# Gated window attention on one Trainium2 core: values projected in front of the row products, and eight-row turns of the maxima

## The chip, the cores and the metric

The kernel runs on 1 core of one Trainium2 (trn2) chip. The metric is the device time in microseconds (us) of one execution. Before the change the median of 3 runs is 1691.44 us (1687.55 to 1694.93).

## What is computed

Eight batches of 512 positions with 256 channels. Each is normalised, projected to 32 query heads and 8 key and value heads of 64, turned by a rotary embedding, and goes through attention in a window of 128 positions to either side with a sink logit for each head. The result is projected back, multiplied by a gate from a small layer with an 8-bit float input, and added to x.

```
xn = layernorm(x)
q, k, v = xn@Wq + bq, xn@Wk + bk, xn@Wv + bv            # q: 32 heads, k and v: 8 heads
q, k = rope(q)*SCALE, rope(k)*SCALE
scores = where(|i - j| <= 128, q.k, -1e9)
probs = softmax(concat(scores, sink))[..., :-1]
s = (probs @ v) @ Wo + bo
scale = max(max(|xn|) / 448, 1e-7)                      # over all eight batches
g = silu(float8((xn / scale)) @ weight.T + bias)
out = x + s * g
```

## The kernel before, in words

The program is written out by hand for each engine; the order of each engine's work is that of its own `step` function, and semaphores order the engines among each other. There are 64 steps, one for each batch n and key head k (step `it` is 8n + k), each with its 4 query heads. A step has 4 slots (q = 0 to 3), one for each tile of 128 query positions. Three stages overlap: in slot q of step `it` TensorE

- projects the queries of step it+2 (`queries`, slot 0 only, two times six matmuls, L1171),
- computes the scores of step `it`, tile q, transposed, in blocks of 128 keys (`scores`, L1253 and L1255; ScalarE takes the exponential of each block, L676, and GpSimd cuts the window's edge, L580),
- computes row products of step it+1 (`score_rows`, L1229, called `row(h)` for the 4 heads), of which VectorE takes the largest value of each row (`maximum`, L988),
- multiplies the exponentials of the tile before with the values (`weighed(h)`, L1269: two blocks of keys make 4 records, three make 6), and VectorE divides by the sums (`normalised`, L997 to L1003),
- turns the heads of the tile before that (`heads_turn`, L1279, two transposes into bank ring[2]), ScalarE and VectorE split the result into a high and a low part (`o_high` L734, `o_low` L1009), and the tile before that one is projected back (`out_project`, L1294).

The softmax needs the maxima as rows that a matmul can add. So two tiles' maxima (4 heads each) are negated (L729), turned by a matmul each into ring[2] (`turn_max`, L1203, in slots 1 and 3), and ScalarE writes 4 rows of 256 columns for each head into `qT_high` (`max_rows`, L711), each with the column of the identity that keeps one head's row and zeroes the others. The second half of `scores` then has 64 + 4 rows. Ring[2] serves both turns: `heads_turn` waits in slots 1 and 3 until `max_rows` has read it, and ScalarE runs `max_rows` in order behind two exponentials.

Once in a while a slot has other work (`chunk_at`): keys of a coming group of four heads, the values of the coming batch (`project_values`, L1180, slots 1 to 3 of step 7, and slot 1 of step 0 for the last tile), transposes of x. In those slots the heads go in the order 0, 2, 1, 3. The values' bank is ring[1], which `row(1)` and `row(3)` also use. `row(0)` of tile 0 waits for the q and k of the step it belongs to, which arrive by DMA.

The opening (step -1) prepares the first batch, surveys all the other batches for the largest |x| (`survey`, `widest`, VectorE and GpSimd), and computes the scale from it. Here the values of tiles 0 to 2 are projected in slots 1 to 3, each ahead of its slot's row products, and VectorE adds their bias ahead of its maxima.

```
                    if it == -1:
                        extra()
                    row(0)
```

## Time and profile before

| | |
|---|---|
| median of 3 runs | 1691.44 us |
| profiled execution, own time | 1689.69 us |
| its span, first to last instruction | 1687.8 us |
| TensorE busy | 1623.2 us, 96% of the span |
| VectorE, ScalarE, GpSimd busy | 68%, 59%, 62% |
| mean granted TensorE clock | 0.979 of full speed |
| one batch (eight steps), from 501 to 702 us | 201 us |

The span is that of the profiled execution; 1.9 us of its time lie around it. PE is TensorE, PEld its weight loads, DVE VectorE, ACT ScalarE, POOL GpSimd. A PE record's own duration includes its way through the array; how much of PE's time it takes is read from the start of one to the start of the next. From about 105 us on the profile repeats with every batch, and ahead of that lies the opening.

### The profile page before, as it was taken

The page shows a single profiled execution, that of the slowest core. Times are in us where ns is not written, and L with a number is a line of the kernel's source. Part 1 is how long each engine was busy: PE and PEld are TensorE (multiplying, and loading weights), DVE is VectorE, ACT ScalarE, POOL GpSimd, SP SyncE. Part 2 cuts the span into 40 slices and gives each one's busy share as a digit, 9 for nine tenths or more (in the row PEclk, how much of TensorE's full clock was granted, in tenths as well). Part 3 has the DMA queues.
Part 4 walks back from the last instruction along what each step waited for, and adds up shares of the span by engine and source line. Part 5 has one row for each costly group of instructions (what it writes and reads, how often), then busy time and mean ns, then how long its engine had stood idle before and what let it go on. Part 6 is the DMA issues. An engine that isn't in the chain of part 4 may idle for free.

```text
span 1687.8 us, 34027 instructions
## 1 busy us (share of the span) xinstructions
PE 1623.2 (96%) x11139; PEld 1459.4 (86%) x11139; DVE 1140.4 (68%) x3619; ACT 991.3 (59%) x2407; POOL 1039.2 (62%) x1016
## 2 busy tenths in 40 slices
PE   3699999999999999999999999999999999999998
PEld 2498988999898998988989898898988899898987
DVE  8656776766766766666676667676676667666664
ACT  2346665566565665566655666556655566555663
POOL 5647675675666666575576666566665666656651
PEclk8679999999999999999999999999999999999999
DMA  6535535435444453534545443643544544443550
GB/s 205 129 73 102 93 69 104 86 78 98 76 88 97 83 98 71 107 70 85 97 77 100 82 88 72 113 82 74 107 72 83 102 77 98 79 79 76 94 97 13
DMA packets 77277, 150.87 MB, mean 89 GB/s; under 512 B 12720, under 2 KB 25264, under 8 KB 73008
## 3 DMA queue, kind: packets, MB, share of 16 engines
q1 hardware_dynamic: 77104, 148.71, 45.6%
q8 instruction: 91, 1.49, 0.4%
q14 instruction: 82, 0.67, 0.2%
HBM read 18.64 MB, written 4.19 MB: 14 GB/s over the span
## 4 chain that ended last, share of the span: by engine, by line
PE 90%; issue 3%; ACT 3%; DVE 2%; POOL 1%; DMA 1%; SPq 0%; POOLq 0%; DVEq 0%; ACTq 0%
PE pv_bank L1269 30%; PE ring L1171 13%; PE ring L1229 11%; PE acc L1294 10%; PE score L1253 9%; PE score L1255 8%; PE ring L1279 4%; PE ring L1180 3%; PE ring L1161 1%; PE ring L1203 1%; ACT qT_high L711 1%; ACT prob_all L676 1%; DMA gate<-in_w_all 1%; PE ring L1141 0%; DVE k_first_hi L966 0%
## 5 line engine op out<-in xcount | busy, mean ns | idle before, releaser
L988 DVE CUSTOM_DVE_ANT_0 junk<-ring,mask,sink 128x384 bf16<-128x384 f32 (+1 forms) x1024 | 558.7, 549 | 306.8 <-PE ring L1229 288.4
L1269 PEld LDWEIGHTS pv_bank<-v,prob_all 128*128 128x128 f32 x5120 | 689.2, 193 | 31.2 <-ACT prob_all L676 11.6
L1269 PE MATMUL pv_bank<-v,prob_all 128*128 128x65 f32 x5120 | 690.9, 266 | 3.6 <-DVE o_norm L1003 1.4
L580 POOL TENSOR_SCALAR_AFFINE_SELECT prob_all<-prob_all 128x512 f32<-128x512 f32 x384 | 255.6, 680 | 456.9 <-ACT prob_all L676 456.9
L676 ACT ACTIVATE prob_all<-score 128x512 f32<-128x512 f32 x640 | 371.5, 596 | 183.1 <-PE score L1255 172.3
L1229 PE MATMUL ring<-kT_high,qT_full 128*128 128x384 f32 (+1 forms) x1024 | 373.3, 365 | 22.6 <-issue 12.0
L1253 PE MATMUL score<-qT_full,kT_high 128*128 128x512 f32 x640 | 265.0, 414 | 0.7
L1255 PE MATMUL score<-qT_high,kT_low 68*128 68x512 f32 x640 | 255.5, 399 | 0.0
L1229 PEld LDWEIGHTS ring<-kT_high,qT_full 128*128 128x128 f32 x1024 | 197.5, 193 | 56.4 <-issue 15.6
L734 ACT ACTIVATE oT_hi<-ring 128x256 fp32r<-128x256 f32 x256 | 96.7, 378 | 179.6 <-PE ring L1279 178.6
L1009 DVE TENSOR_TENSOR oT_lo<-ring,oT_hi 128x256 fp32r<-128x256 f32 x256 | 107.9, 422 | 137.1 <-ACT oT_hi L734 135.4
L711 ACT ACTIVATE qT_high<-ring,ident 4x256 fp32r<-4x256 f32 x512 | 196.4, 452 | 5.9 <-PE ring L1203 2.6
L1294 PE MATMUL acc<-wo_hi,oT_hi 128*128 128x256 f32 x512 | 155.4, 304 | 0.2 <-DVE oT_lo L1009 0.2
L540 POOL TENSOR_TENSOR q_first<-q_first,q_first_hi 128x512 f32<-128x512 f32 x64 | 83.8, 1309 | 115.6 <-ACT q_first_hi L693 115.6
L1294 PE MATMUL acc<-wo_hi,oT_lo 128*128 128x256 f32 x512 | 143.4, 280 | 0.0
L1294 PE MATMUL acc<-wo_lo,oT_hi 128*128 128x256 f32 x512 | 143.3, 280 | 0.0
L1171 PE MATMUL ring<-xT_hi,w_hi 128*128 128x512 f32 x320 | 129.5, 405 | 12.3 <-ACT q_even L682 8.3
L1253 PEld LDWEIGHTS score<-qT_full,kT_high 128*128 128x128 f32 x640 | 122.3, 191 | 15.3 <-ACT prob_all L676 1.8
L1171 PE MATMUL ring<-xT_hi,w_lo 128*128 128x512 f32 x320 | 127.5, 398 | 0.0
L1171 PE MATMUL ring<-xT_lo,w_hi 128*128 128x512 f32 x320 | 127.3, 398 | 0.0
L1255 PEld LDWEIGHTS score<-qT_high,kT_low 68*128 68x128 f32 x640 | 121.9, 191 | 2.7
L682 ACT ACTIVATE q_even<-ring,q_bias 128x512 f32<-128x512 f32 x64 | 44.1, 689 | 129.9 <-PE ring L1171 129.9
(127 smaller groups left out, 2570.2 us busy)
## 6 DMA issues: line engine op xcount, KB each, us to landing
qT_high<-qT_full SPq DMA_DIRECT2D x64, 512.0 KB, 4.5
qT_full<-q_first SPq DMA_DIRECT2D x64, 256.0 KB, 4.2
qT_full<-q_first_hi SPq DMA_DIRECT2D x64, 256.0 KB, 5.5
qT_full<-q_second SPq DMA_DIRECT2D x64, 256.0 KB, 4.2
qT_full<-q_second_hi SPq DMA_DIRECT2D x64, 256.0 KB, 5.4
kT_high<-k_first_hi SPq DMA_DIRECT2D x128, 64.0 KB, 2.5
kT_high<-k_second_hi SPq DMA_DIRECT2D x128, 64.0 KB, 2.7
x_res<-in_x SPq DMA_DIRECT2D x10, 512.0 KB, 6.2
```

Source lines behind the costliest of these rows:

```text
L580: nc.gpsimd.affine_select(out=pr, in_=pr, compare_op=ALU.is_ge, fill=0.0, base=0, pattern=[[0, GROUP], [sign, P]], channel_multiplier=-sign) \
L676: nc.scalar.activation(prob[:, q % 2 * 3 + n, :], score[(FIRST[q] + n) % 2][:, :], ACT.Exp) \
L711: last = nc.scalar.activation(qT_high[D:D + NR, s % 2, h, pair * 2 * P:(pair + 1) * 2 * P], ring[2][0:NR, 0:2 * P], ACT.Copy, scale=ident[ ...
L734: nc.scalar.activation(oT_hi[:, q % 2, :], ring[2][:, 0:KT * P], ACT.Copy).then_inc(s_oT_hi_done, 1)
L988: nc.vector.tensor_tensor_reduce(junk[:, h % 2, 0:cols], ring[h % 2][:, 0:cols], mask[:, m0:m0 + cols], 1.0, sink[:, col:col + 1], ALU.add ...
L1009: nc.vector.tensor_tensor(oT_lo[:, q % 2, :], ring[2][:, 0:KT * P], oT_hi[:, q % 2, :].bitcast(F32), ALU.subtract).then_inc(s_oT_lo_done, 1)
L1171: last = nc.tensor.matmul(bank[:, :], w[:, k, col:col + P], xs[:, k, :], start=(n == 0), stop=(n == len(products) - 1))
L1229: nc.tensor.matmul(ring[h % 2][:, 0:cols], qT_full[:, b % 2, h, q * P:(q + 1) * P], kT_high[:, b % 3, k0 * P:k0 * P + cols], start=True, s ...
L1253: nc.tensor.matmul(score[blk % 2][:, :], kT_high[:, c % 3, k * P:(k + 1) * P], qT_full[:, c % 2, :, q * P:(q + 1) * P], start=True, stop=F ...
L1255: nc.tensor.matmul(score[blk % 2][:, :], kT_low[0:D + NR, c % 3, k * P:(k + 1) * P], qT_high[0:D + NR, c % 2, :, q * P:(q + 1) * P], start ...
L1269: last = nc.tensor.matmul(pv[:, h, :], prob[:, q % 2 * 3 + n, h * P:(h + 1) * P], v[:, slot, k, :], start=(n == 0), stop=(n == len(BLOCKS[ ...
L1294: last = nc.tensor.matmul(acc[q // 2][:, (q % 2) * M:(q % 2 + 1) * M], left[:, q % 2, k * P:(k + 1) * P], right[:, col:col + M], start=fre ...
```

## The change

Four things change.

1. The maxima of two tiles are turned by one matmul into eight rows (`NR` is 8). `max_rows` then issues eight ACTIVATEs of 8 rows by 128 columns where it issued four of 4 by 256. `scores` has 72 rows in its second half.
2. In slots 1 and 3 `heads_turn` follows `weighed(3)`; VectorE's `normalised` goes ahead of `o_low` there, and in slot 1 ahead of `maximum` 3.
3. In slot 1 of step 7 TensorE projects the values ahead of `row(0)`, and VectorE adds their bias ahead of that row's maximum.
4. In the opening the values of tiles 0 to 2 are projected at once into ring[1], score[0] and score[1], ahead of all row products, and their bias is added ahead of all maxima. 32 matmuls whose result nobody reads (`turn_over`) stand ahead of step -1, and 12 behind the values.

```diff
-NR = GROUP
+NR = 2 * GROUP
@@ max_rows (ACT)
-                for h in range(GROUP):
-                    last = nc.scalar.activation(qT_high[D:D + NR, s % 2, h, pair * 2 * P:(pair + 1) * 2 * P],
-                                                ring[2][0:NR, 0:2 * P], ACT.Copy, scale=ident[0:NR, h:h + 1])
+                for t in range(2):
+                    for h in range(GROUP):
+                        i, q = t * GROUP + h, 2 * pair + t
+                        last = nc.scalar.activation(qT_high[D:D + NR, s % 2, h, q * P:(q + 1) * P],
+                                                    ring[2][0:NR, 2 * P:3 * P], ACT.Copy, scale=ident[0:NR, i:i + 1])
@@ step (DVE)
-                    if it < 0 and other is not None:
-                        values(other[1], other[2])
+                    if (it, q) == (-1, 0):
+                        for t in range(TILES - 1):
+                            values(0, t)
+                    first = (k, q) == (KV - 1, 1) and it >= 0 and other is not None
+                    if first:
+                        values(other[1], other[2])
...
-                    if real(back(it, q, 2)[0]):
+                    if q % 2 == 0 and real(back(it, q, 2)[0]):
                         o_low(*back(it, q, 2))
+                    if q == 1 and real(back(it, q, 1)[0]):
+                        normalised(*back(it, q, 1))
                     if real(r) and order[1] == 2 and q < 3:
                         maximum(r, tile, 3, order)
-                    if real(back(it, q, 1)[0]):
+                    if q != 1 and real(back(it, q, 1)[0]):
                         normalised(*back(it, q, 1))
+                    if q % 2 and real(back(it, q, 2)[0]):
+                        o_low(*back(it, q, 2))
@@ turn_max (PE)
-                for t in range(2):
-                    last = nc.tensor.matmul(ring[2][0:NR, t * P:(t + 1) * P], neg_parts[:, pair, t, :], ident_r[:, :],
-                                            start=True, stop=True)
-                last.then_inc(s_max_turned_pe, 1)
+                nc.tensor.matmul(ring[2][0:NR, 2 * P:3 * P], neg_parts[:, pair, :], ident_r[:, :],
+                                 start=True, stop=True).then_inc(s_max_turned_pe, 1)
@@ step (PE)
-                    if it == -1:
-                        extra()
-                    row(0)
+                    first = (k, q) == (KV - 1, 1) and it >= 0 and other is not None
+                    if not first:
+                        row(0)
...
+                    if it == -1 and q == 0:
+                        pe.wait_ge(s_odd_done, 2)
+                        project_values(0, ring[1])
+                        project_values(1, score[0])
+                        project_values(2, score[1])
+                        turn_over(12)
                     maxima_turn()
                     if heads_at(it, q)[1] == 2:
                         if it >= 0:
                             extra()
+                        if first:
+                            row(0)
                         weighed(0)
                         third()
                         row(2)
                         weighed(1)
                         row(1)
                         weighed(2)
-                        heads_turn()
                         if q == 3:
                             row(3)
                             weighed(3)
+                            heads_turn()
+                        elif q == 1:
+                            weighed(3)
+                            heads_turn()
+                            row(3)
                         else:
+                            heads_turn()
                             weighed(3)
                             row(3)
...
+            def turn_over(count):
+
+                for _ in range(count):
+                    nc.tensor.matmul(acc[1][:, :], ident_r[:, :], xT_hi[:, 0, :], start=True, stop=True)
```

TensorE, slot 1 of a step without other work (step 3 of the first batch). Names are tiles: `ring<-kT_high,qT_full` is a row product, `ring<-ident,o_norm` the turn of the heads, `pv_bank` the product with the values. Before:

```order
L1229 MATMUL ring<-kT_high,qT_full 128x256 [waits max_done]
L1269 MATMUL pv_bank<-v,prob_all 128x65 x2
L1229 MATMUL ring<-kT_high,qT_full 128x256 [waits max_done]
L1269 MATMUL pv_bank<-v,prob_all 128x65 x2
L1279 MATMUL ring<-ident,o_norm 128x128 [waits oT_lo_done,norm_done,max_rows_done]
L1279 MATMUL ring<-ident,o_norm 128x128
L1269 MATMUL pv_bank<-v,prob_all 128x65 x2
L1294 MATMUL acc<-wo_hi,oT_hi 128x256 [waits oT_lo_done]
```

and of the change, at the same place:

```order
L1246 MATMUL ring<-kT_high,qT_full 128x256 [waits max_done]
L1288 MATMUL pv_bank<-v,prob_all 128x65 x2
L1246 MATMUL ring<-kT_high,qT_full 128x256 [waits max_done]
L1288 MATMUL pv_bank<-v,prob_all 128x65 x4
L1298 MATMUL ring<-ident,o_norm 128x128 [waits oT_lo_done,norm_done,max_rows_done]
L1298 MATMUL ring<-ident,o_norm 128x128
L1313 MATMUL acc<-wo_hi,oT_hi 128x256 [waits oT_lo_done]
```

The turn of the maxima, some rows above, was two matmuls (L1203, 4x128 each) and is one (L1219, 8x128). The last head's product with the values stands ahead of the heads' turn instead of behind it.

TensorE, slot 1 of step 7 in the first batch, before:

```order
L1255 MATMUL score<-qT_high,kT_low 128x512
L1229 MATMUL ring<-kT_high,qT_full 128x256 [waits kT_high_in,max_done,qT_second_in,qT_first_in]
L1253 MATMUL score<-qT_full,kT_high 128x512 [waits exp_done]
L1255 MATMUL score<-qT_high,kT_low 128x512
L1203 MATMUL ring<-ident_r,neg_parts 4x128 [waits max_rows_done,neg_done,oT_lo_done]
L1203 MATMUL ring<-ident_r,neg_parts 4x128
L1180 MATMUL ring<-w_hi,xT_hi 128x512 [waits max_done]
```

and of the change:

```order
L1274 MATMUL score<-qT_high,kT_low 128x512
L1219 MATMUL ring<-ident_r,neg_parts 8x128 [waits max_rows_done,neg_done,oT_lo_done]
L1192 MATMUL ring<-w_hi,xT_hi 128x512 [waits max_done]
L1192 MATMUL ring<-w_lo,xT_hi 128x512
L1192 MATMUL ring<-w_hi,xT_lo 128x512
L1192 MATMUL ring<-w_hi,xT_hi 128x512
L1192 MATMUL ring<-w_lo,xT_hi 128x512
L1192 MATMUL ring<-w_hi,xT_lo 128x512
L1246 MATMUL ring<-kT_high,qT_full 128x256 [waits kT_high_in,max_done,qT_second_in,qT_first_in]
L1288 MATMUL pv_bank<-v,prob_all 128x65 [waits norm_done,cut_done,exp_done]
```

The row product that waits for the DMAs of q and k stands behind both scores, the turn of the maxima and the six matmuls of the values.

VectorE in the opening, of the change, behind the sixth survey (`L977` and `L980` are the values' bias, `L992` the maxima, `L845` the seventh survey):

```order
L852 BN_AGGR x_moments<-stats 128x2 [waits row_bn] x4
L977 TENSOR_TENSOR v<-ring,v_bias 128x7x64 [waits v_pe]
L980 TENSOR_TENSOR v<-ring,v_bias 128x64
L977 TENSOR_TENSOR v<-score,v_bias 128x7x64 [waits v_pe]
L980 TENSOR_TENSOR v<-score,v_bias 128x64
L977 TENSOR_TENSOR v<-score,v_bias 128x7x64 [waits v_pe]
L980 TENSOR_TENSOR v<-score,v_bias 128x64
L992 ISA junk,row_max<-ring,mask,sink 128x256 [waits max_pe]
L992 ISA row_max 128x1
```

The three values stand in a row ahead of the first maximum; before, each stood ahead of the four maxima of its slot.

## Rows read from the trace of the kernel before

**Rows 1.** The page, part 1: each engine's busy time

```profile
PE 1623.2 (96%) x11139; PEld 1459.4 (86%) x11139; DVE 1140.4 (68%) x3619; ACT 991.3 (59%) x2407; POOL 1039.2 (62%) x1016
```

**Rows 2.** Busy time by stretch: opening, cold stretch, one batch (PE, PEld, DVE, ACT, POOL, PEclk)

```profile
44.75:62.53 17.78, 12.09 (x25) 7.14 (x25) 12.32 (x43) 7.62 (x16) 17.26 (x12) 0.50 0.96 203
82.00:100.00 18.00, 18.00 (x76) 16.50 (x77) 7.18 (x27) 7.64 (x19) 10.59 (x11) 0.50 0.13 22
501.00:702.00 201.00, 199.14 (x1393) 180.06 (x1393) 138.04 (x443) 122.17 (x300) 127.04 (x124) 1.00 0.46 87
```

**Rows 3.** Waits of TensorE from 110 to 1680 us: total us, times, longest

```profile
PE ring L1229 <- issue: 8.4, 7, 2.1
```

**Rows 4.** Timeline, PE, slot 1 of a plain step: start us, duration us

```profile
517.85 0.55 PE L1269 MATMUL pv_bank<-v,prob_all 128*128 128x65 f32 x4
518.37 0.44 PE L1279 MATMUL ring<-ident,o_norm 128*128 128x128 f32 x2
518.64 0.56 PE L1269 MATMUL pv_bank<-v,prob_all 128*128 128x65 f32 x4
519.01 0.37 PE L1294 MATMUL acc<-wo_hi,oT_hi 128*128 128x256 f32 x1
```

**Rows 5.** Timeline, ACT, the same slot

```profile
516.78 1.53 ACT L711 ACTIVATE qT_high<-ring,ident 4x256 fp32r<-4x256 f32 x4
```

**Rows 6.** Timeline, ACT, the two smallest copies of 128 columns

```profile
4.51 0.31 ACT L647 ACTIVATE ident_b<-ident 128x128 bf16<-128x128 f32 x1 [2.44 <-POOL mask L491]
4.73 0.29 ACT L648 ACTIVATE ident_r<-ident 128x128 fp32r<-128x128 f32 x1
```

**Rows 7.** Groups of ACT by shape: busy us, mean ns of one

```profile
L676 ACT ACTIVATE prob_all<-score 128x512 f32<-128x512 f32 x640 | 371.5, 596 | 183.1 <-PE score L1255 172.3
L711 ACT ACTIVATE qT_high<-ring,ident 4x256 fp32r<-4x256 f32 x512 | 196.4, 452 | 5.9 <-PE ring L1203 2.6
L720 ACT ACTIVATE sink_exp<-neg_parts,sink 128x2 f32<-128x2 f32 x512 | 108.2, 285 | 0.1
...
L682 ACT ACTIVATE q_even<-ring,q_bias 128x512 f32<-128x512 f32 x64 | 44.1, 689 | 129.9 <-PE ring L1171 129.9
```

**Rows 8.** Timeline, ACT, slot 3 of a plain step

```profile
503.67 1.53 ACT L711 ACTIVATE qT_high<-ring,ident 4x256 fp32r<-4x256 f32 x4
```

**Rows 9.** Timeline, PE, the same slot 3

```profile
505.50 0.39 PE L1279 MATMUL ring<-ident,o_norm 128*128 128x128 f32 x2
```

**Rows 10.** Timeline, PE, slot 1 of a step 7

```profile
461.32 0.40 PE L1255 MATMUL score<-qT_high,kT_low 68*128 68x512 f32 x1
462.77 0.36 PE L1229 MATMUL ring<-kT_high,qT_full 128*128 128x256 f32 x1 [1.05 <-issue]
...
463.43 0.28 PE L1203 MATMUL ring<-ident_r,neg_parts 128*4 128x128 f32 x2
463.55 0.44 PE L1180 MATMUL ring<-w_hi,xT_hi 128*128 128x512 f32 x1
...
464.99 0.55 PE L1269 MATMUL pv_bank<-v,prob_all 128*128 128x65 f32 x4
...
465.90 0.28 PE L1229 MATMUL ring<-kT_high,qT_full 128*128 128x256 f32 x1
```

**Rows 11.** Timeline, PE, slot 3 of a step 7

```profile
480.48 0.39 PE L1279 MATMUL ring<-ident,o_norm 128*128 128x128 f32 x2
480.90 0.44 PE L1229 MATMUL ring<-kT_high,qT_full 128*128 128x384 f32 x1
```

**Rows 12.** Timeline, DVE, the opening

```profile
44.75 0.59 DVE L973 TENSOR_TENSOR v<-ring,v_bias 128x448 f32<-128x448 f32 x1
...
45.39 0.47 DVE L988 CUSTOM_DVE_ANT_0 junk<-ring,mask,sink 128x256 bf16<-128x256 f32 x1
...
58.74 0.63 DVE L973 TENSOR_TENSOR v<-ring,v_bias 128x448 f32<-128x448 f32 x1 [3.02 <-PE ring L1180]
```

**Rows 13.** Timeline, POOL, the opening

```profile
55.31 2.28 POOL L507 TENSOR_TENSOR x_rstd<-x_var,minus_half_all 128x12 f32<-128x12 f32 x1
```

More of the change, by code:

```diff
@@ L971, in values @@
                 dve.wait_ge(s_v_pe, TILES * m + t + 1)
+                bank = score[t - 1] if m == 0 and t in (1, 2) else ring[1]
                 last = KV - 1 + m % 2
                 nc.vector.tensor_tensor(v[:, 0:KV - 1, t, 0:D],
-                                        ring[1][:, 0:(KV - 1) * D].rearrange("p (g d) -> p g d", d=D),
+                                        bank[:, 0:(KV - 1) * D].rearrange("p (g d) -> p g d", d=D),
                                         v_bias[:, 0:(KV - 1) * D].rearrange("p (g d) -> p g d", d=D), ALU.add)
-                nc.vector.tensor_tensor(v[:, last, t, 0:D], ring[1][:, (KV - 1) * D:], v_bias[:, (KV - 1) * D:],
+                nc.vector.tensor_tensor(v[:, last, t, 0:D], bank[:, (KV - 1) * D:], v_bias[:, (KV - 1) * D:],
                                         ALU.add).then_inc(s_v_done, 1)
@@ L1091, in step @@
                         beside(it, n, k, q)
-                    if other is not None and it >= 0:
+                    if other is not None and it >= 0 and not first:
                         if other[0] == "k":
@@ L1179, in project_values @@
                 for n, (xs, w, k) in enumerate(products):
-                    last = nc.tensor.matmul(ring[1][:, :], xs[:, k, t * P:(t + 1) * P], w[:, k, W_V:W_V + KV * D],
+                    last = nc.tensor.matmul(bank[:, :], xs[:, k, t * P:(t + 1) * P], w[:, k, W_V:W_V + KV * D],
                                             start=(n == 0), stop=(n == len(products) - 1))
                 last.then_inc(s_v_pe, 1)
+            def turn_over(count):
+                for _ in range(count):
+                    nc.tensor.matmul(acc[1][:, :], ident_r[:, :], xT_hi[:, 0, :], start=True, stop=True)
             def queries(a, odd):
@@ L1214, in score_rows @@
                         pe.wait_ge(s_odd_done, 1)
-                if h == 1:
-                    other = chunk_at(it // KV, it % KV, slot)
+                if h == 1 and b == 0 and q == 0:
+                    pe.wait_ge(s_v_done, 1)
+                elif h == 1:
+                    other = chunk_at(it // KV, it % KV, slot) if it >= 0 else None
                     if slot == 0 and real(it + 2):
@@ L1315, in other_chunk @@
                 elif kind == "v":
-                    if i == 0 and j == 0:
-                        pe.wait_ge(s_odd_done, 2)
-                    if i == 0 and j > 0:
-                        pe.wait_ge(s_v_done, j)
-                    project_values(j)
+                    project_values(j, ring[1])
                 elif kind == "x":
@@ L1446, in _ @@
             queries(0, 1)
+            turn_over(32)
             for it in range(-1, STEPS + 1):
```

16 lines of the change are left out of this document (11 added, 5 removed).

## The prediction

> **What bounds the kernel now.** I read the page first, then the busy time by stretch, then the waits of TensorE, and then the timelines of TensorE, ScalarE and VectorE slot by slot. The page has TensorE busy for 96% of the span, 28 points ahead of VectorE, the next engine [rows 1]. The stretch of one batch says it more sharply: 199.14 of 201 us at the full clock [rows 2]. So from 105 us on every matmul taken away is time gained, as long as no other engine ends the slot, and every wait put into TensorE's stream is lost. The waits have one large entry there: seven times a row product waits for something that is no engine, 8.4 us in all [rows 3]. Those are the DMAs of q at the step between two batches. Small waits hide in the array's tail, so I take them from start to start. In slot 1 of a plain step the third head's product starts at 517.85 and is good for 0.37 us (as the fourth's from 518.64 to 519.01), so the turn of the heads could start at 518.22; it starts at 518.37 [rows 4], just after the last of the four ACTIVATEs that read ring[2] ends (516.78 + 1.53 = 518.31) [rows 5]. So in this slot ScalarE already sets the pace by 0.15 us. The profile shows this in steps 1 to 5 of each batch, 40 slots in all; in slot 1 of steps 0, 6 and 7, with their six extra matmuls, ScalarE is done 0.9 us or more before. Ahead of 105 us VectorE is the bound of the opening: between 44.75 and 62.53 us it is busy 12.32 of 17.78 us, with TensorE at half clock [rows 2].
>
> **One matmul for the turn.** Two matmuls take 0.12 us from 463.43 to 463.55 [rows 10]; one takes 0.06. That saves 0.06 us in 128 turns, but in the 40 slots where ScalarE sets the pace it saves nothing: 88 x 0.062 = **5.5 us less**.
>
> **Eight ACTIVATEs for four.** No row shows an ACTIVATE of 128 columns with a scale read from memory, one after the other. From four of 256 columns (mean 0.452, four in 1.53) their spacing is (1.53 - 0.45) / 3 = 0.36 us; for 2 columns with a pointer it is (4 x 0.211 - 0.285) / 3 = 0.19 [rows 7]. Half-way between lies 0.28. The other route: a plain copy of 128 columns takes 0.29 to 0.31 with a spacing of 0.22 [rows 6], and a pointer operand adds 0.09 (0.689 for q_even against 0.596 for the exponential, both 512 columns) [rows 7]: 0.29 to 0.31. Bounds: 0.22 if the pointer is free, 0.36 if 128 columns cost as much as 256. I take 0.28, as both routes end near it: 7 x 0.28 + 0.38 = 2.34 us for the eight, 0.81 us more than now. In the 40 slots the last head's product now stands ahead of the turn, so TensorE is ready at 518.22 - 0.06 + 0.37 = 518.53; ScalarE ends at 516.78 + 2.34 = 519.12, so the turn starts at 519.17, and the back projection 0.27 us later at 519.44 instead of 519.01: 0.43 us. **40 x 0.43 = 17.2 us more.** The reordering thus pays 0.37 of the 0.81. In slot 3 ScalarE ends at 505.20 and the turn starts at 505.50 [rows 8, 9]; it moves to 505.50 - 0.06 + 0.59 = 506.03 against 506.01 + 0.05. That is even; in step 6, where the margin is 0.17 instead of 0.30, it lacks 0.15. With rounding in the others: **2 us more**.
>
> What waits behind the longer ACTIVATEs on ScalarE: the third exponential, four small ones for the sinks and the high part of the heads. They come 0.8 us later, and TensorE's next score, 0.4 later as well, finds ScalarE just free. VectorE's `o_low` waits for that high part; that `normalised` now stands ahead of it is what keeps the product's bank from being late. I cost these moves at nothing; if the cover fails, the next maximum is late by some tenths in the same 40 slots.
>
> By the Trainium skill ("ScalarE: Activation LUTs", section on what ACT_TABLE_LOAD costs) an ACTIVATE takes 186 ns + 0.833 ns a column, each pointer operand adds 93 ns, and neighbours overlap by 93 ns. That fits the row of 2 columns (279 + 2 = 281 against 285 ns), while for 256 columns it gives 492 ns against the 452 of the trace. As an estimate by that page, eight of 128 columns take 7 x 0.293 + 0.386 = 2.44 us, and the sum below comes out some 8 us higher.
>
> **Values ahead of `row(0)`, seven times.** The row product starts 1.45 us after the score before it, which needs 0.23: 1.22 us of wait, of which the list shows 1.05 [rows 10]. Over seven that makes 8.4 + 7 x 0.17 = 9.6 us. The second score, the turn and the values (463.55 to 464.99, 1.44 us) now stand there, 1.96 us in all; only the longest wait of 2.1 + 0.17 leaves 0.3. The values move the load: VectorE adds the bias first (44.75 to 45.39, 0.64 us) and then takes the maximum (0.47) [rows 12]. With 0.2 us to start, my estimate, the maximum is there 1.35 us after the values' last matmul. `row(2)`, which needs it, would be ready after row(0)'s 0.12 and the 0.91 from 464.99 to 465.90 [rows 10], 1.03 in all. A new wait of 0.32, seven times 2.3. Net **-9.6 + 0.3 + 2.3, about 6.9 us less**. What is late next here is VectorE.
>
> **Slot 3 with other work (steps 1, 5, 7).** Here row(3) waits for a maximum, and the turn of the heads fills part of that wait: 480.48 to 480.90 is 0.42 us, of which the turn takes some 0.24 (0.27 where it follows a wait) [rows 4, 11]. Behind the change row(3) is issued at the same time, since VectorE sets it, and the turn comes afterwards: 0.24 us in each of 23 such slots, **5.5 us more**.
>
> **The opening.** VectorE idles 17.78 - 12.32 = 5.46 us between 44.75 and 62.53 [rows 2]. 3.02 of it is the wait for tile 2's values, which TensorE projects late and at half clock [rows 12]; the rest is the start of pairs of maxima behind the values. With all values first, both row products are ready when VectorE comes to them. I leave 0.3 for the turn of the first maxima in slot 3: **5.2 us less**. Next in line is GpSimd's last 1/sqrt, done at 55.31 + 2.28 = 57.6 [rows 13]; the new end, 57.3 plus the 1.1 us for the reduction of x, lies behind it. The 44 idle matmuls lie ahead of row products that cannot be served before VectorE is free at 44.75, and I cost them at nothing: 32 of them take 7.4 us (0.23 each) in a wait of over 8. If the clock were at half, values and fillers would end near 49 us, and 2.5 of the 5.2 would be gone.
>
> **Sum.** -5.5 + 17.2 + 2 - 6.9 + 5.5 - 5.2 = +7.1 us. The profiled execution took 1689.7 us, so 1696.8; it lies 1.7 us under the median of the runs, so against the median that is 1698.5. I forecast **1697**. About 0.5%, 8.5 us, is what a measurement of this kernel can tell from no change: the forecast is at the upper edge of no change.
>
> **Rivals.**
> 1. *ScalarE's spacing is 0.29 or more.* One mechanism, in slots 1 of steps 1 to 5 and then in slots 3. For it speak the copies plus pointer. At 0.29 the eight take 2.42 us, 0.08 more: 40 x 0.08 + 32 x 0.08 + 8 x 0.08 = 6.4, in all +13.5: **1703**, slower by 0.8%. The sum passes +8.5 with less than 0.003 us more of spacing than I took. Were it 0.36, it would be 0.6 us more in all 80 slots: some 50 us, which nothing but the bound speaks for.
> 2. *The spacing is 0.22, the pointer free when in a row.* The eight take 1.85; ScalarE ends at 518.63, TensorE waits 0.15 as now and saves the rest. 17.2 and 2 vanish and 2 come back: -14: **1676**, faster by 0.8%. Against it: 0.19 for only 2 columns.
> 3. *The clock.* After the opening TensorE runs at half clock from 82 to beyond 100 us though busy all the time [rows 2], behind a wait of 2.5 us. If other timing of the opening avoids that, the 18 us alone give back 9: **1688**, no change; if it comes once more, 1706.
> 4. *The fillers or the banks do not keep the opening short*: half of the 5.2 lost, **1699.5**.
>
> **Chances.** Forecast and what lies around it 0.42; it lies near the edge, so 0.10 of that is slower and 0.32 within 0.5%. Rival 1 0.22, slower. Rival 2 0.16, faster. Rival 3 0.12, a third each: the better clock with cheap ACTIVATEs (faster), with the forecast's (within), and the worse one (slower). Rival 4 0.08, 0.03 of it slower. That makes faster 0.20, within 0.5% 0.41, slower 0.39. The range from 1680 to 1710 leaves out most of rival 2 and the far end of rival 1, at most 0.2 together.
>
> **What would show it.** The ACTIVATEs of 8 x 128: spacing 0.28, eight in 2.3 us. Slot 1 of steps 1 to 5: turn of the heads 0.6 us behind the last product. Slot 1 of step 7: no wait at row(0), a small one at row(2). Slot 3 of steps 1, 5, 7: 0.24 more before row(3). VectorE from the first value to the reduction of x in 12.6 us instead of 17.8. A batch takes 202.5 us instead of 201. If the eight take under 2.1 us, or the batch is at or below 201, my term for ScalarE is wrong; if the opening gains nothing, the one for VectorE.

## The result and the profile after

| | before | after |
|---|---|---|
| median of 10 runs each, on the same chip | 1688.13 us | 1680.52 us |
| lowest and highest | 1683.89, 1694.93 | 1677.29, 1686.64 |
| ratio to before, 95% interval | | 0.9955 [0.9941, 0.9969] |
| profiled execution (span) | 1689.69 us (1687.8) | 1686.64 us (1684.7) |
| a batch, from `q_even` to `q_even` eight steps later | 201.0 us | 200.1 us |

The change takes 7.6 us off, 0.45%. The forecast was 1697, 0.5% up: the sign is wrong. The profiled execution after is the slowest of its ten, so the two profiled spans differ by 3 us where the medians differ by 7.6. Most of this lies in the first batch, which takes 213.4 us before and 217.4 after, and 207.6 to 220.0 in the profiled executions of the experiments. From the second batch on the traces of both kernels repeat within 0.2 us (but for the seventh before, 202.1 us, with the longest wait for q), so I read the change there.

Two things lengthen the first batch after. When step 1 starts, the changed kernel is 6.4 us ahead (first score at 99.96 against 106.35 us). There VectorE stands for x of the coming batch, `gate` is queued behind that, and TensorE's turn of the heads waits for `gate`; the kernel before comes later and has no such wait of TensorE:

```profile
106.91 0.75 DVE L817 BATCH_NORM_STATS2 stats<-x_in 128x6 f32<-128x256 f32 x2 [5.53 <-DMA x_in<-in_x]
107.58 0.67 DVE L912 TENSOR_TENSOR gate<-ring,ffn_bias 128x512 f32<-128x512 f32 x1
```

```profile
108.31 0.69 PE L1298 MATMUL ring<-ident,o_norm 128*128 128x128 f32 x2 [3.27 <-DVE gate L912]
```

Then the granted clock goes to half from 107.8 to 121.4 us, and slot 1 of step 1 takes 8.64 us instead of 4.89. Nine of the fourteen traces of this document have this wait of TensorE, 2.6 to 3.3 us long.

The page after, part 1 (each engine's busy time; answers to [rows 1]), and part 4 (the chain that ended last) by engine:

```profile
PE 1620.2 (96%) x11055; PEld 1463.0 (87%) x11055; DVE 1151.2 (68%) x3619; ACT 1064.5 (63%) x2919; POOL 1036.7 (62%) x1016
...
PE 80%; ACT 9%; DVE 6%; issue 3%; DMA 1%; POOL 1%; SPq 0%; POOLq 0%; DVEq 0%; ACTq 0%
```

The same line of part 4 before:

```profile
PE 90%; issue 3%; ACT 3%; DVE 2%; POOL 1%; DMA 1%; SPq 0%; POOLq 0%; DVEq 0%; ACTq 0%
```

ScalarE is busy 73 us longer than in [rows 1], and has gone from 3% of the chain to 9%. The chain names a new pacemaker, not a loss: the time fell.

Busy time of the engines after, in a stretch of one batch (columns as in [rows 2]):

```profile
501.00:702.00 201.00, 198.52 (x1388) 180.21 (x1386) 139.80 (x445) 131.81 (x365) 126.55 (x124) 1.00 0.47 88
```

TensorE idles 2.5 us in it, where [rows 2] had 1.9. Waits of TensorE, from 110 to 1680 us (in all, times, longest), after:

```profile
PE ring L1246 <- DVE row_max L992: 6.9, 28, 0.3
PE ring L1298 <- ACT qT_high L713: 4.5, 17, 0.4
PE ring L1246 <- issue: 2.0, 1, 2.0
PE pv_bank L1288 <- DVE o_norm L1007: 1.9, 8, 0.2
```

and two lines of the same list before, beside [rows 3]:

```profile
PE ring L1279 <- ACT qT_high L711: 2.2, 9, 0.3
PE pv_bank L1269 <- DVE o_norm L1003: 1.4, 4, 0.4
```

The wait for q [rows 3] fell from 8.4 us to 2.0. Of its seven places before, six are slot 1 of step 7 (7.2 us), and these are gone; the seventh, and the one that is left, is slot 1 of step 6 in the last batch, where it grew from 1.2 to 2.0. Two small waits came up: one for a maximum, 28 times, and the one for the ACTIVATEs, 17 times where it stood 9 times. A matmul's record runs on while it passes through the array, and a start that is late by less than that tail leaves no idle time in this list. So the ledger is better made slot by slot, from the first score of a slot to the first score of the next, medians over batches 3 to 7 (us):

| slots | before | after | change | forecast |
|---|---|---|---|---|
| slot 1 of steps 1, 3, 4, 5 | 4.89 | 5.02 | +0.13 | +0.43 |
| slot 1 of step 2 | 5.46 | 5.59 | +0.13 | +0.43 |
| slot 2 of steps 2, 3, 4 | 5.95 | 5.65 | **-0.30** | 0 |
| slot 1 of step 7 | 7.39 | 6.52 | -0.87 | -1.0 |
| slot 3 of steps 1, 5 | 8.68 | 8.80 | +0.12 | +0.18 |
| slot 3 of step 7 | 8.43 | 8.55 | +0.12 | +0.18 |
| slot 3 of steps 0, 2, 3, 4 | 6.74 | 6.68 | -0.06 | 0 |
| slot 1 of steps 0, 6 | 6.12, 6.40 | 6.05, 6.33 | -0.07 | -0.06 |

Over all 32 slots of a batch the changes add up to -1.0 us (slot 2 of step 1 rose by 0.10); the period of a batch fell by 0.9.

**Slot 1.** Timeline after, TensorE and then ScalarE, in the slot of [rows 4, 5] (start, duration):

```profile
518.79 1.00 PE L1288 MATMUL pv_bank<-v,prob_all 128*128 128x65 f32 x8
519.94 0.44 PE L1298 MATMUL ring<-ident,o_norm 128*128 128x128 f32 x2
520.13 0.37 PE L1313 MATMUL acc<-wo_hi,oT_hi 128*128 128x256 f32 x1
```

```profile
517.78 2.11 ACT L713 ACTIVATE qT_high<-ring,ident 8x128 fp32r<-8x128 f32 x8
519.91 0.60 ACT L676 ACTIVATE prob_all<-score 128x512 f32<-128x512 f32 x1
```

The group of ACT by shape (busy us, mean ns of one):

```profile
L713 ACT ACTIVATE qT_high<-ring,ident 8x128 fp32r<-8x128 f32 x1024 | 269.9, 343 | 3.3
```

Eight take 2.11 us with a mean of 0.343, so they follow one another at (2.11 - 0.343) / 7 = 0.252 us. The turn starts 0.05 us behind the last, as forecast, but it is 0.23 us less late. The back projection starts 0.19 us behind the turn (519.94, 520.13), where the forecast had 0.27; that is the rest of the difference between +0.13 and +0.43.

**Slot 2, where the forecast has nothing.** VectorE before, then after, at the start of slot 2 of step 2 (its first score starts at 547.44 before, at 548.89 after):

```profile
547.63 0.42 DVE L1009 TENSOR_TENSOR oT_lo<-ring,oT_hi 128x256 fp32r<-128x256 f32 x1 [1.56 <-ACT oT_hi L734]
...
548.37 0.43 DVE L1003 TENSOR_TENSOR o_norm<-pv_bank,rden 128x256 f32<-128x256 f32 x1
```

```profile
548.47 0.42 DVE L1007 TENSOR_TENSOR o_norm<-pv_bank,rden 128x256 f32<-128x256 f32 x1 [0.42 <-PE ring L1298]
549.53 0.42 DVE L1013 TENSOR_TENSOR oT_lo<-ring,oT_hi 128x256 fp32r<-128x256 f32 x1 [0.63 <-ACT oT_hi L737]
```

TensorE before, then after: the second row product of the slot and the first product with the values:

```profile
548.54 0.34 PE L1229 MATMUL ring<-kT_high,qT_full 128*128 128x384 f32 x1
548.94 0.63 PE L1269 MATMUL pv_bank<-v,prob_all 128*128 128x65 f32 x4
```

```profile
550.00 0.34 PE L1246 MATMUL ring<-kT_high,qT_full 128*128 128x384 f32 x1
550.17 0.78 PE L1288 MATMUL pv_bank<-v,prob_all 128*128 128x65 f32 x6
```

Before, VectorE stands for 1.56 us in front of `o_low`, which needs ScalarE's high part, and `o_norm`, which empties the products' bank, is queued behind it. It ends at 548.80, and the first product follows at 548.94, 0.40 us behind the row product, which is good for 0.17. After, `o_norm` is done at the slot's start, and the product follows at 0.17 us. That wait of 0.23 us or more was there in the trace before, and I had not laid VectorE's rows of this slot beside TensorE's. The list of waits has no entry for this slot, but it had a hint: the line on `pv_bank` above names the same pair of VectorE and TensorE, in slot 3 of step 6 of the first batch and at three places of the last.

### The profile page after: what moved, and what is told of

Read it like the earlier page. It is cut to its first block, busy times and chain, and to the rows that moved or that the text cites. A ratio compares the mean times of both kernels' runs of the same rounds, so it can differ in the third digit from the quotient of the medians.

```text
span 1684.7 us, 34367 instructions
## 1 busy us (share of the span) xinstructions
PE 1620.2 (96%) x11055; PEld 1463.0 (87%) x11055; DVE 1151.2 (68%) x3619; ACT 1064.5 (63%) x2919; POOL 1036.7 (62%) x1016
## 4 chain that ended last, share of the span: by engine, by line
PE 80%; ACT 9%; DVE 6%; issue 3%; DMA 1%; POOL 1%; SPq 0%; POOLq 0%; DVEq 0%; ACTq 0%
PE pv_bank L1288 24%; PE ring L1183 13%; PE acc L1313 10%; PE ring L1246 9%; PE score L1272 8%; PE score L1274 7%; ACT qT_high L713 5%; PE ring L1298 4%; ACT prob_all L676 3%; PE ring L1192 2%; DVE junk L992 2%; PE ring L1173 1%; DVE k_first_hi L969 1%; DMA gate<-in_w_all 1%; PE ring L1153 0%
## 5 line engine op out<-in xcount | busy, mean ns | idle before, releaser
L992 DVE CUSTOM_DVE_ANT_0 junk<-ring,mask,sink 128x384 bf16<-128x384 f32 (+1 forms) x1024 | 561.1, 550 | 318.7 <-PE ring L1246 300.2
L1288 PE MATMUL pv_bank<-v,prob_all 128*128 128x65 f32 x5120 | 677.8, 267 | 1.9 <-DVE o_norm L1007 1.9
L713 ACT ACTIVATE qT_high<-ring,ident 8x128 fp32r<-8x128 f32 x1024 | 269.9, 343 | 3.3
L1274 PE MATMUL score<-qT_high,kT_low 72*128 72x512 f32 x640 | 256.6, 401 | 0.0
L1274 PEld LDWEIGHTS score<-qT_high,kT_low 72*128 72x128 f32 x640 | 123.0, 192 | 2.9
L1007 DVE TENSOR_TENSOR o_norm<-pv_bank,rden 128x256 f32<-128x256 f32 x256 | 108.7, 425 | 16.9 <-PE ring L1298 9.2
```

Of the source, the lines that this page charges most:

```text
L713: last = nc.scalar.activation(qT_high[D:D + NR, s % 2, h, q * P:(q + 1) * P], ring[2][0:NR, 2 * P:3 * P], ACT.Copy, scale=ident[0:NR, i:i ...
L992: nc.vector.tensor_tensor_reduce(junk[:, h % 2, 0:cols], ring[h % 2][:, 0:cols], mask[:, m0:m0 + cols], 1.0, sink[:, col:col + 1], ALU.add ...
L1007: nc.vector.tensor_tensor(o_norm[:, :, :], pv[:, :, 0:D], rden[:, :].rearrange("p (h a) -> p h a", a=1).broadcast_to([P, GROUP, D]), ALU.m ...
L1274: nc.tensor.matmul(score[blk % 2][:, :], kT_low[0:D + NR, c % 3, k * P:(k + 1) * P], qT_high[0:D + NR, c % 2, :, q * P:(q + 1) * P], start ...
L1288: last = nc.tensor.matmul(pv[:, h, :], prob[:, q % 2 * 3 + n, h * P:(h + 1) * P], v[:, slot, k, :], start=(n == 0), stop=(n == len(BLOCKS[ ...
```

## Experiments

Twelve kernels; "-" and "+" are against the kernel named, and "..." marks lines that are left out. Slot times are medians over batches 3 to 7 of one profiled execution. A gain in us of a kernel's time is against the median of the kernel before on the same chip; such a difference is good to about 3 us, that of `e1_eight` and `e8_low_first` to some 7.

**One part at a time, from the kernel before.** `e1_eight`: the eight-row turn alone.

```
-NR = GROUP
+NR = 2 * GROUP
...
+                nc.tensor.matmul(ring[2][0:NR, 2 * P:3 * P], neg_parts[:, pair, :], ident_r[:, :],
+                                 start=True, stop=True).then_inc(s_max_turned_pe, 1)
```

> The kernel before with the eight-row turn alone, its heads' turn still ahead of the last head's product. The changed kernel's trace has eight ACTIVATEs in 2.11 us against four in 1.53, 0.58 us more. Theory (ScalarE ends slots 1 and 3, and the cover of the reordering is what makes the eight rows bearable): in slot 1 of steps 1 to 5 TensorE loses the whole 0.58, in slot 3 of steps 0, 2, 3, 4 and 6, where 0.30 or 0.17 us were to spare, 0.33 to 0.45; together some 4.7 us a batch, 37 us in all, less 0.06 for each turn that stands free. Rival (the ACTIVATEs lie beside other work anyway): within 5 us of before.

Measured: 1727.56 us over two executions, ratio 1.0218 [1.0174, 1.0262], 37.6 us slower. Slot 1 of steps 1 to 5 +0.57 each, slot 3 of steps 0, 2, 3, 4 +0.38, slot 2 of step 6 +0.43, and slot 1 of step 7 gives 1.36 back. In slot 3 of step 6 it is +0.85 in the second batch and +4.0 in the fourth to seventh. Busy time by stretch of that slot, fourth and second batch:

```profile
861.03:872.20 11.17, 10.28 (x50) 8.99 (x49) 7.05 (x18) 5.78 (x18) 8.58 (x7) 0.69 0.69 109
450.70:458.69 7.99, 7.11 (x50) 6.08 (x49) 7.07 (x18) 5.66 (x18) 7.49 (x7) 1.00 0.54 101
```

The same 50 matmuls, but the granted clock goes to 0.5 from 865.2 to 872.0 us, and so once in each of these four batches, 3.2 us a time. TensorE stood idle for 0.9 us of the slot either way. So a half-clock stretch can fall into the steady part as well; 13 of the 37.6 us are of that kind. That the sum met the expected 37 us is therefore luck: without the stretches a batch takes 4.0 us more, not 4.7. The eight rows alone cost five times what the whole change gained.

`e2_sums_first`: VectorE's order alone.

```
-                    if real(back(it, q, 2)[0]):
+                    if q % 2 == 0 and real(back(it, q, 2)[0]):
                         o_low(*back(it, q, 2))
+                    if q == 1 and real(back(it, q, 1)[0]):
+                        normalised(*back(it, q, 1))
...
```

> The kernel before with VectorE's order of slots 1 and 3 alone: the sums' division ahead of the heads' low part. Theory (the 0.29 us that slot 2 of steps 2, 3 and 4 lost in the changed kernel is this order, since the product with the values waited for the one bank until VectorE had first waited for ScalarE's high part): slot 2 of steps 2, 3 and 4 falls from 5.95 to 5.65 us, nothing else moves, 0.9 us a batch, 7 us in all. Rival (it is TensorE's order, the last head's product ahead of the turn, that lets the division come early): slot 2 stays at 5.95 and the time as before.

Measured: 1682.83 us, ratio 0.9958 [0.9939, 0.9977], -7.1 us. Slot 2 of steps 2, 3, 4: 5.95 to 5.66; of step 5: -0.09; nothing else moves by more than 0.04. The order that I costed at nothing is worth, within 3 us, as much as the whole change.

`e3_step7`: the values ahead of `row(0)` in step 7 alone.

```
-                    row(0)
+                    first = (k, q) == (KV - 1, 1) and it >= 0 and other is not None
+                    if not first:
+                        row(0)
...
```

> The kernel before with the values ahead of row(0) in slot 1 of step 7 alone. Theory (the values cover the DMA, and VectorE's bias gives a third of a us back): that slot falls from 7.39 to some 6.58 us, seven times, 6 us in all. Rival (what the changed kernel gained there came from the shorter wait behind the turn): under 2 us in all.

Measured: 1683.85 us, ratio 0.9962 [0.9945, 0.9978], -6.1 us; slot 1 of step 7 7.39 to 6.59, no other slot. (In the first batch no wait for q stood in that slot, and it rises from 6.13 to 6.58.) This trace too has a half-clock stretch in the steady part, from 250.1 to 256.9 us, without the eight rows.

`e4_opening`: the opening alone, with its three banks and its 44 idle matmuls.

```
-                    if it == -1:
-                        extra()
+                    if it == -1 and q == 0:
...
+                        project_values(0, ring[1])
+                        project_values(1, score[0])
+                        project_values(2, score[1])
+                        turn_over(12)
...
```

> The kernel before with the opening's change alone (three banks, values first, 44 idle matmuls). Theory (VectorE reaches the reduction of x 3.7 us earlier, but its product with 1/sqrt then meets GpSimd's work and takes 2.3 us instead of 0.2): the scale is ready 2 us earlier than before, and the time is 2 us lower give or take the clock's stretches of 4 us. Rival (my prediction): the scale is ready 5.2 us earlier. Second rival: the gain of the changed kernel over ten runs comes from a clock that stays up longer in the opening, then this kernel alone is 5 us or more faster.

Measured: 1690.61 us, ratio 1.0002 [0.9982, 1.0022]. The scale of x is ready at 65.0 us instead of 66.6, and no gain shows in the time; the interval of some 4 us to either side would still hold one of 2 us. Here TensorE waits 2.9 us for `gate` in step 1, which the kernel before does not.

`e12_turn_later`: TensorE's order alone, in slot 1 the turn of the heads behind the last head's product. The edit moves it in slot 3 of steps 0, 2, 3, 4 and 6 too, as the whole change does.

```
...
-                        heads_turn()
+                        if q % 2 == 0:
+                            heads_turn()
                         weighed(3)
+                        if q % 2:
+                            heads_turn()
```

> This is the kernel before with one thing changed in TensorE's order: in slot 1 the turn of the heads stands behind the last head's product. Four rows, VectorE's old order and the old step 7 stay. Theory (the reordering pays only together with VectorE's new order, because the high part of the heads comes later and the low part, which VectorE has first, holds up the normalised heads): slot 1 of steps 1, 4 and 5 falls from 4.89 to 4.72 and that of step 2 from 5.46 to 5.02, but slot 2 of steps 2 to 5 rises from 5.95 by 0.1 to 0.3; net -0.4 to +0.3 us in a batch, time within 3 us of the kernel before, ratio 0.998 to 1.002. Rival (the two orders are independent): slot 2 keeps its times, a batch takes 0.9 us less, 7 us in all, ratio near 0.996.

Measured: 1686.43 us, ratio 0.9993 [0.9978, 1.0008]: nothing, as the theory has it (-1.5 us, less than its interval). Slot 1 of steps 1, 3, 4, 5 -0.17 and of step 2 -0.45; slot 2 of step 2 +0.44, of steps 3, 4, 5 +0.17, of step 6 +0.31; slot 3 of step 6 +0.87, most of which slot 1 of step 7 gives back (-1.27), as q has arrived by then. VectorE and TensorE in the slot shown above:

```profile
544.63 0.42 DVE L1009 TENSOR_TENSOR oT_lo<-ring,oT_hi 128x256 fp32r<-128x256 f32 x1 [1.56 <-ACT oT_hi L734]
...
545.37 0.42 DVE L1003 TENSOR_TENSOR o_norm<-pv_bank,rden 128x256 f32<-128x256 f32 x1
```

```profile
545.94 0.63 PE L1269 MATMUL pv_bank<-v,prob_all 128*128 128x65 f32 x4 [0.50 <-ACT prob_all L676]
```

The product starts 0.15 us behind the end of `o_norm` (545.79), as it does before (548.80, 548.94). The profile names ScalarE's exponential, whose second one happens to end at the same time; before, the product started at 548.94 while that second one ran from about 548.7 to 549.33, so it is not what the product needs.

**One part taken back, from the changed kernel.** `e5_four_rows`: two matmuls and four ACTIVATEs of 256 columns again, all else as changed.

```
-NR = 2 * GROUP
+NR = GROUP
...
```

> This is the changed kernel with the old turn of the maxima: two matmuls into four rows and four ACTIVATEs of 256 columns, all else as changed. Theory (the eight rows cost time even under the new order, since the turn of the heads has to wait for the longer ACTIVATEs): the four take 1.53 us instead of 2.11, ScalarE is done before the last product's end, slot 1 of steps 1 to 5 goes from 5.02 to about 4.7 us (5 a batch, 8 batches: -12 us), and the second matmul of the turn costs 0.06 in 128 turns (+8): about 4 us below the changed kernel, ratio to the kernel before near 0.993. Rival (the one matmul saved is worth more than the wait, so the eight rows carry the gain): slower than the changed kernel by some 5 us, ratio to the kernel before near 0.999.

Measured: 1670.77 us, ratio 0.9891 [0.9876, 0.9906], some 11 us below the changed kernel: the theory's sign, at over twice its size. TensorE and ScalarE in slot 1 of a plain step:

```profile
512.70 1.00 PE L1287 MATMUL pv_bank<-v,prob_all 128*128 128x65 f32 x8
513.54 0.39 PE L1297 MATMUL ring<-ident,o_norm 128*128 128x128 f32 x2
513.68 0.37 PE L1312 MATMUL acc<-wo_hi,oT_hi 128*128 128x256 f32 x1
```

```profile
511.63 1.53 ACT L711 ACTIVATE qT_high<-ring,ident 4x256 fp32r<-4x256 f32 x4
```

ScalarE is done at 513.16, and the turn waits for nothing: 0.84 us behind the start of the eight products, where the changed kernel has 1.15. Slot 1 of steps 1, 4, 5 takes 4.72 us, that of step 2 5.02 (changed kernel: 5.59), that of step 3 5.02, as now `row(0)` waits for the DMAs of q: it starts at 560.73, 0.04 us behind SyncE's next DMA (560.69), which waits for the same q, and VectorE's last maximum has ended by 560.29. A batch takes 199.2 us: 0.9 less than changed, 7 us over eight. In the two profiled executions, 15.5 us apart, the rest lies in the first and the last batch (5.8 and 5.1 us apart, 0.9 of each by the slots); in the last the changed kernel has a half-clock stretch from 1636.9 to 1643.8 us and this one has none. The eight rows aren't what decides on that stretch: `e7_row3_after` (eight rows) has none there, `e11_four_row3` (four) has one from 1620.1 to 1627.0. In the four traces that have one there, it begins 0.9 to 1.8 us behind a wait of TensorE of 1.5 to 2.0 us, the one for q in slot 1 of step 6. The six traces in which this wait is 1.2 us have none, but four with a wait of 1.6 to 2.0 have none either, so what decides is open.

`e8_low_first`: VectorE's old order back.

```
-                    if q % 2 == 0 and real(back(it, q, 2)[0]):
+                    if real(back(it, q, 2)[0]):
                         o_low(*back(it, q, 2))
-                    if q == 1 and real(back(it, q, 1)[0]):
-                        normalised(*back(it, q, 1))
...
```

> This is the changed kernel with VectorE's old order: the low part of the heads ahead of the normalised heads. Theory (the gain of the changed kernel is VectorE's order, and with the longer ACTIVATEs the high part of the heads comes later still): slot 2 of steps 2 to 4 goes back from 5.65 to 5.95 us or beyond, up to 6.5, and slot 2 of the other steps may lose too; 24 x 0.3 to 24 x 0.8, so 7 to 20 us slower than the changed kernel, ratio to the kernel before 1.000 to 1.008. Rival (the order is worth its 7 us only beside the old turn of the maxima): within 2 us of the changed kernel.

Measured: 1716.49 us, ratio 1.0160 [1.0126, 1.0194]: some 35 us above the changed kernel, more than the theory gave. Slot 2 of steps 2, 3, 4 6.39 (5.65 with the new order), of steps 5 and 6 +0.40, slot 3 of step 6 +0.82: 3.9 us in a batch (204.0), 207.1 in two of them, where again a half-clock stretch of 6.8 us falls in. In the slot shown above:

```profile
556.11 0.43 DVE L1013 TENSOR_TENSOR oT_lo<-ring,oT_hi 128x256 fp32r<-128x256 f32 x1 [2.13 <-ACT oT_hi L737]
...
556.85 0.42 DVE L1007 TENSOR_TENSOR o_norm<-pv_bank,rden 128x256 f32<-128x256 f32 x1
```

```profile
557.42 0.85 PE L1284 MATMUL pv_bank<-v,prob_all 128*128 128x65 f32 x6 [0.50 <-ACT prob_all L676]
```

The idle time in front of `o_low` is 2.13 us, and the product starts 0.15 us behind `o_norm` for the third time.

`e7_row3_after`: in slot 3 of steps 1, 5, 7 the turn of the heads ahead of `row(3)` again.

```
                         if q == 3:
+                            heads_turn()
                             row(3)
                             weighed(3)
-                            heads_turn()
```

> This is the changed kernel with the turn of the heads ahead of row(3) again in slot 3 of steps 1, 5 and 7. Theory (row(3) waits there for its maximum, and the turn of the heads fills that wait): these slots lose the 0.11 to 0.17 us that they gained, 23 x 0.15 = 3.5 us, ratio to the kernel before near 0.9935. Rival (the turn of the heads now waits for the longer ACTIVATEs in that place and holds up row(3)): no change or up to 3 us slower than the changed kernel.

Measured: 1677.17 us, ratio 0.9936 [0.9910, 0.9961]. The three slots go from 8.80, 8.79 and 8.55 to 8.61, 8.60 and 8.38, all others stay; a batch takes 199.5 us. That is 0.55 us, some 4 over eight. The time's interval overlaps the changed kernel's; the slots show the gain.

`e9_pool_waits`: GpSimd's last products held back.

```
-            for n in range(5, FFN_CHUNK + 1):
+            chunk_low(5)
+            pool.wait_ge(s_amax_done, 1)
+            for n in range(6, FFN_CHUNK + 1):
```

> This is the changed kernel with GpSimd's products for the low parts of the last weight chunks held back until VectorE has the scale of x. Theory (in the opening VectorE's small product of x and the 1/sqrt takes 2.27 us instead of 0.22 because GpSimd works beside it): the product takes about 0.2 us, inv_scale is ready near 62.7 us instead of 64.7, q_even of step 0 starts near 65.7 instead of 67.7, and the time falls by up to 2 us, which the clock of the opening may hide. Rival (the product is long for another reason, as a late input): it keeps its 2.27 us and the scale its time. Second rival (GpSimd's late products are needed early): the first steps get longer by what GpSimd is late, 2 us or more.

Measured: 1678.39 us, ratio 0.9935 [0.9917, 0.9954]; not told apart from the changed kernel. VectorE and GpSimd in the changed kernel's opening, and VectorE here:

```profile
60.42 2.27 DVE L866 TENSOR_TENSOR x_ends<-x_ends,x_rstd 128x56 f32<-128x56 f32 x1
```

```profile
60.28 2.34 POOL L514 TENSOR_TENSOR wo_lo<-gate,wo_hi 128x1024 fp32r<-128x1024 f32 x1
```

```profile
60.25 0.22 DVE L868 TENSOR_TENSOR x_ends<-x_ends,x_rstd 128x56 f32<-128x56 f32 x1
```

With GpSimd silent the product takes 0.22 us, and the scale is ready at 62.5 us instead of 64.7. Theory and trace agree; a gain of 2 us is smaller than what the two times can tell apart. The lead of 2.2 us is again followed by TensorE's wait for `gate` (2.9 us).

`e6_no_fillers`: without the 44 matmuls that nobody reads.

```
-                        turn_over(12)
...
-            turn_over(32)
```

> This is the changed kernel without the 44 matmuls in the opening whose result nobody reads (32 of them behind the first queries, 12 behind the values). Theory (they run in a wait, and no row shows a gain by them): VectorE's first value comes at the same time, and the time is within 4 us of the changed kernel, ratio to the kernel before near 0.9955, however the stretches at half clock fall. Rival (they keep the clock up when the values are projected): without them TensorE's values between 35 and 39 us and its row products behind them run at half clock, the scale of x comes 1 to 3 us later, ratio 0.9965 to 0.999. Second rival (they are what brings the clock down between 46 and 70 us): up to 8 us faster, ratio 0.991.

Measured: 1682.14 us, ratio 0.9955 [0.9939, 0.9971], as the changed kernel. Half clock in its profiled execution from 29.0 to 35.8 and 42.7 to 70.0 us, against 46.3 to 70.2 with them; the reduction of x starts at 58.97 instead of 58.84. In all eight traces with the fillers the clock stays at full to 44.7 us or beyond, in the six without it falls at 27.0 to 29.0. So the fillers keep the clock up for a time in which TensorE mostly waits, and a gain from it, if any, is below 3 us.

**Both kernels beaten.** `e11_four_row3`: `e5_four_rows` with the edits of `e7_row3_after` and `e9_pool_waits`.

> This is the kernel with four rows everywhere, and the turn of the heads ahead of row(3) again in slot 3 of steps 1, 5 and 7, and GpSimd's late products held back. Theory (row(3) waits for its maximum there, so the turn of the heads is free ahead of it): these slots go from 8.85, 8.86 and 8.61 to 8.68, 8.68 and 8.43, 0.5 us in a batch, 4 us in all; near 1667 us, ratio near 0.987. Rival (no gain, because VectorE's last product in the slot is then later for the next slot): 1670 us, ratio 0.989.

Measured: 1665.85 us, ratio **0.9859** [0.9841, 0.9876], 22 us below the kernel before; a batch 198.7 us, slot 3 of steps 1, 5, 7 8.67, 8.68, 8.43.

`e10_mixed`: the same, but with the eight-row turn in slot 3 and the four-row turn in slot 1.

> This is the changed kernel with each form of the maxima's turn where it costs least: in slot 3 one matmul and eight ACTIVATEs of 128 columns, in slot 1 two matmuls and four ACTIVATEs of 256 columns; the turn of the heads ahead of row(3) again in slot 3 of steps 1, 5 and 7; and GpSimd's late products held back until the scale of x is there. Theory (the parts add up): slot 1 of steps 1, 4 and 5 at 4.72 and of step 2 at 5.02 as with four rows, slot 3 of steps 0, 2, 3 and 4 at 6.68 as with eight, slot 3 of steps 1, 5, 7 at 8.61, 8.61 and 8.38; a batch takes 198.4 us, 0.8 less than with four rows everywhere, and the time is near 1664 us, ratio to the kernel before near 0.985. Rival (the two forms in turns disturb each other, as the first ACTIVATEs of a slot then wait for the other region of the bank): 1670 us or more, ratio 0.989 or above.

Measured: 1669.35 us, ratio 0.9887 [0.9868, 0.9906]. By the slots the parts add up (slot 3 of steps 0, 2, 3, 4 6.69 beside 4.72 in slot 1), a batch takes 198.5 us, 0.2 less than `e11_four_row3`; the time is no better. Its first batch took 215.8 us against 211.0, with 27.3 us at half clock between 77 and 120 us against 17.1. The expectation of 1664 was missed and the time lies near the rival's (0.989); but no slot shows the two forms disturbing each other. Why its opening keeps the lower clock is open.

## Why the prediction was wrong

Two steps failed: a mechanism that the sum had at nothing, and the price of the eight ACTIVATEs.

- **"I cost these moves at nothing"** is the step whose mechanism was missed. I had seen that `normalised` ahead of `o_low` keeps the bank from being late under the longer ACTIVATEs, and took it for a cover. It is a gain: the bank was already late before, in slot 2 of three steps. `e2_sums_first` gives it -7.1 us. And the cover is worth more than "some tenths in the same 40 slots": without it the changed kernel loses some 35 us (`e8_low_first`), some 6 of them in two half-clock stretches.
- **The term for the eight ACTIVATEs** was the largest error in us: 17.2 forecast, 5.2 measured (+0.13 in 40 slots, where +0.43 stood). Of the 0.30, 0.23 is the spacing (0.28 taken, 0.252 measured): the eight cost 0.58 us more, not 0.81. The other 0.07 to 0.08 is that the back projection starts 0.19 us behind the turn, not 0.27. Slot 3's "2 us more" is a gain of 0.06 in each of its plain slots. 0.252 lies between rival 2's 0.22 and the forecast. By the Trainium skill ("ScalarE: Activation LUTs", section on what ACT_TABLE_LOAD costs) the spacing would be 0.293 and one would take 386 ns; the trace has 0.252 and 343 ns, 41 to 43 ns below it on both. The sign of the term was right: `e5_four_rows` shows that the eight rows are dear.
- **The pair of orders.** I let TensorE's new order pay 0.37 of the 0.81. By itself it pays nothing (`e12_turn_later`): what slot 1 gains, slot 2 loses, as the high part is later and VectorE's old order hands that on. With both orders and four rows slot 1's gain stays, but for step 3, and slot 2 of steps 2 to 6 loses nothing by it (`e5_four_rows`, 19.0 us below the kernel before). The parts alone give 7.1 + 6.1 + 1.5; the 4 us between are no more than the intervals allow. That the orders act together is shown by the slots, not by this sum.
- **Step 7** came out near its price, -6.9 forecast, -6.1 measured alone, with a residual wait of VectorE's kind at `row(2)`, as described. The reading behind it was not quite right: the list's seven waits are not seven steps 7, and the one in step 6 of the last batch grew by 0.8.
- **Slot 3 with other work** was right in kind and 1.3 times too large: +0.17 to +0.19 where 0.24 stood.
- **The opening** was wrong in size: -5.2 forecast, no gain measured within some 4 us. VectorE does finish the maxima 3.7 us earlier (58.84 for 62.53), but then its small product meets GpSimd's and waits for its end (2.27 us for 0.22), so the scale is ready only 1.9 us earlier. What is left of the lead is lost in step 1 of the profiled execution, by the wait for `gate` and at half clock; that the same happens in the others is likely, not shown. I had named GpSimd's last 1/sqrt as next in line, and not the product behind it.
- **Fillers at nothing**: not contradicted, within 3 us.

The changes of the slots add up to -1.0 us a batch or -8 in all, and -7.6 is the result; in the two profiled executions batches 2 to 7 give -6.6 us, and the first and last are moved by clock and waits. With the two measured sizes of the ScalarE term alone my sum would read -5.5 + 5.2 + 0 - 6.9 + 5.5 - 5.2 = -6.9, and that it meets the result would be luck: the 5.2 us of the opening didn't show, and VectorE's 7 us stood nowhere. Rival 2 gave the nearest time (1676) for a reason that was half right, and its nearness rests in part on the same luck; nothing in my list held VectorE's order.

## What to carry to other kernels

When a diff moves an instruction of an engine that isn't the bound, lay that engine's rows beside the bound engine's in every slot where it moves, and look for a start of the bound engine at a fixed distance (here 0.14 to 0.15 us) behind the moved instruction's end: a wait shorter than the array's tail has no row in the list of waits. Cut an edit into its orders and its costs before it is judged: here a loss (38 us by itself, some 7 to 11 beside the new orders), two gains of 6 and 7 us and an order worth nothing by itself were one change of 0.45%. Fewer instructions on the bound engine did not pay here, as they doubled those of the engine that releases it.

## What the runs showed of the hardware

- VectorE's TENSOR_TENSOR of 128x56 with both inputs in SBUF takes 0.22 us by itself and 2.27 us when it starts 0.14 us behind a GpSimd TENSOR_TENSOR (60.28 + 2.34 = 62.62; VectorE's ends at 62.69). A reduction of 1024 columns (1.22 us) beside GpSimd's products keeps its time. In `e6_no_fillers` the subtraction before it is hit first, ending 0.07 us behind GpSimd's as well:

```profile
60.10 2.40 DVE L864 TENSOR_TENSOR x_ends<-x_ends,x_moments 128x56 f32<-128x56 f32 x1
```

```profile
60.08 2.35 POOL L514 TENSOR_TENSOR wo_lo<-gate,wo_hi 128x1024 fp32r<-128x1024 f32 x1
```

By the Trainium skill ("SBUF — State Buffer", section on the two separate sides) a VectorE operation with two inputs in SBUF and a GpSimd operation that reads SBUF lock a shared pair of ports for the whole instruction, and the later one blocks. The cases above agree with that.
- The granted clock can go to half for 6.8 us in the steady part too, at the same place in four batches in a row (`e1_eight`), though TensorE waits less than 1 us in that slot; `e3_step7` has one such stretch and `e8_low_first` two, each in the same slot, slot 3 of step 6.
- A matmul with 8 columns of weights takes what one with 4 takes (226 and 224 ns, 0.06 us of TensorE's time each), so two tiles' maxima do turn at the price of one.
